# First attention with its two half-seen key blocks merged into one before the softmax

## The reference, cut to what matters

```python
scores = jnp.einsum('bqhgd,bshd->bhgqs', qg, k) * sm_scale
allowed = (j <= i) & (j > i - SLIDING_WINDOW)
scores = jnp.where(allowed[None, None, None], scores, neg)
attn = jax.nn.softmax(scores, axis=-1)
out = jnp.einsum('bhgqs,bshd->bqhgd', attn, v).reshape(B, S, N_Q_HEADS * HEAD_DIM)
return out @ wo
```

## Time and profile before

| what | before |
|---|---|
| median of 3 runs | 2206.22 us (2202.36 to 2208.6) |
| the profiled execution: its own time | 2204.66 us |
| its span, first to last instruction | 2202.8 us |
| mean granted TensorE clock | 0.995 |
| first attention, passes of `kv_head` | about 62 to 692 us of the span |

### The profile page before, as it was taken

One profiled execution on the slowest core, in us unless ns is written; L12 is line 12 of the kernel. 1 busy time (PEld: TensorE's weight loads), 2 busy tenths in 40 slices (PEclk: granted clock), 3 DMA queues, 4 the chain that ended last, 5 costly groups with the idle time before them and its releaser, 6 DMA issues.

```text
span 2202.8 us, 41666 instructions
## 1 busy us (share of the span) xinstructions
PE 2151.4 (98%) x11084; PEld 1653.8 (75%) x11084; DVE 1700.4 (77%) x3415; ACT 1460.7 (66%) x2868; POOL 1232.4 (56%) x1091
## 2 busy tenths in 40 slices
PE   7999999999999999999999999999999999999988
PEld 5888888888887657777777777777777777777756
DVE  6777777777777668888888888888888877788865
ACT  3444444445444668888888888888888877777742
POOL 5656655665653446666666666666666620455334
PEclk9999999999999999999999999999999999999999
DMA  7011010010004142111111111111111111433341
GB/s 245 20 48 30 19 48 29 19 48 29 19 10 125 40 176 82 43 48 49 46 49 42 49 46 48 42 49 46 49 42 48 47 49 42 124 92 111 87 126 39
DMA packets 125422, 132.20 MB, mean 60 GB/s; under 512 B 33205, under 2 KB 75733, under 8 KB 125348
## 3 DMA queue, kind: packets, MB, share of 16 engines
q1 hardware_dynamic: 121508, 118.70, 18.1%
q0 software_dynamic: 3840, 12.59, 1.9%
HBM read 101.46 MB, written 29.10 MB: 59 GB/s over the span
## 4 chain that ended last, share of the span: by engine, by line
PE 92%; DVE 4%; ACT 1%; SPq 1%; issue 1%; POOL 0%; DMA 0%; DVEq 0%; ACTq 0%; POOLq 0%
PE bank L2464 12%; PE bank L2451 11%; PE bank L2471 11%; PE bank L2036 9%; PE bank L2038 9%; PE bank L2037 9%; PE bank L2492 6%; PE bank L2383 5%; PE bank L2382 5%; PE bank L2381 5%; PE bank L2489 2%; PE bank L2172 2%; DVE rope_b L1535 1%; DVE rope_b L1536 1%; DVE rope_a L1534 1%
## 5 line engine op out<-in xcount | busy, mean ns | idle before, releaser
L1817 DVE TENSOR_REDUCE mcol<-bank 128x1 fp32r<-128x512 f32 x1024 | 693.9, 689 | 221.6 <-PE bank L2451 211.2
L2464 PE MATMUL bank<-q,k 128*128 128x512 f32 x1024 | 418.8, 409 | 0.1
L2451 PE MATMUL bank<-km,q 128*128 128x512 f32 x1024 | 405.7, 397 | 2.9 <-DVE mcol L1817 1.6
L2471 PE MATMUL bank<-q,k 128*128 128x512 f32 x1024 | 406.2, 397 | 0.0
L2451 PEld LDWEIGHTS bank<-km,q 128*128 128x128 f32 x1024 | 316.2, 309 | 52.3 <-DVE mcol L1817 4.2
L1329 ACT ACTIVATE pT<-bank 128x512 f32<-128x512 f32 x512 | 284.5, 600 | 81.6 <-PE bank L2471 77.8
L1329 ACT ACTIVATE x<-bank 128x512 f32<-128x512 f32 x512 | 284.6, 600 | 80.8 <-PE bank L2471 77.0
L2464 PEld LDWEIGHTS bank<-q,k 128*128 128x128 f32 x1024 | 192.2, 188 | 127.0 <-ACT x L1329 44.3
L2471 PEld LDWEIGHTS bank<-q,k 128*128 128x128 f32 x1024 | 192.3, 188 | 32.4
L2383 PE MATMUL bank<-hT_hi,wr_lo 128*128 128x512 f32 x512 | 202.9, 396 | 0.0
L2381 PE MATMUL bank<-hT_hi,wr_hi 128*128 128x512 f32 x512 | 200.7, 392 | 1.6 <-DVE k L1690 1.6
(11 more groups left out here) (348 smaller groups left out, 5045.6 us busy)
## 6 DMA issues: line engine op xcount, KB each, us to landing
wst<-in_L_attn_Wq_rope SPq DMA_DIRECT2D x64, 256.0 KB, 3.0
o_d<-ost SPq DMA_DIRECT2D x504, 32.0 KB, 1.8
st_q<-in_L_attn_wq SPq DMA_DIRECT2D x8, 1024.0 KB, 7.4
st_wo<-in_L_attn_wo SPq DMA_DIRECT2D x8, 1024.0 KB, 5.2
km<-kc_d SPq DMA_DIRECT2D x256, 32.0 KB
q<-qc_d SPq DMA_DIRECT2D x256, 32.0 KB
k<-kc_d SPq DMA_DIRECT2D x256, 32.0 KB
wm<-in_L_wmod SPq DMA_DIRECT2D x6, 1024.0 KB, 9.3
```

The source lines that it names most:

```text
L1817: dve.tensor_reduce(mcol[:, k % 2, i % 4, i // 4:i // 4 + 1], bank[4 + i % 2][:], AX.X, ALU.max, negate=True)\
L2451: pe.matmul(bank[4 + i % 2][:], q2[:, k % 4, h, i % 4:S:4], km[:, b, h], start=True, stop=True).then_inc(max_mm, 1)
L2464: pe.matmul(bank[s % 4][:], k1[:, k % 2, t], q1[:, k % 4, h], start=True, stop=False)
L2471: pe.matmul(bank[s % 4][:], k2[:, k % 2, h, t], q2[:, k % 4, h], start=False, stop=True).then_inc(scores1, 1)
```

## The change

The two half-seen blocks are merged while the scores are in the banks: where the first block's place is not seen, the second block's score is copied over it (`copy_predicated`, predicate from the window mask read as integers). From then on a slot has 128 columns a head, not 256. Maximum, exponential and normalising work on the banks; the exponential is written back into the bank. One block is turned, into bank 2 or 3 by the parity of qb. The turned weights P hold both blocks; the output is V_before * P + (V_own - V_before) * (P where own), so the differences of neighbouring V blocks (`dv_hi`, `dv_lo`) are made once a pass, and `pT_hi[:, 1]`, `pT_lo[:, 1]` are P's parts times the 0/1 tile `own` (on DVE and on POOL). There are still six matmuls a slot. For qb = 0 the mask stays as it was; the exponential reads `probs` and writes the bank. `scores` now waits for `probs0` (normalised) of the slot before, not for `masked0`. The lists of `kv_head` are reordered on all four engines, and the last pass on DVE; SP loads one more tile of 64 KB (`own`), and some small tiles change place in SBUF. The second layer's wait on `kr_split` becomes one on `kv_split`.

```diff
 POOL
+            def own_weights(slot):
+                mine = own[:].unsqueeze(1).broadcast_to([P, GQ, P])
+                pool.wait_ge(pT_split, 2 * slot + 1)
+                pool.tensor_tensor(heads(pT_lo[:, 1]), heads(pT_lo[:, 0].bitcast(F32)), mine, ALU.mult).then_inc(pT_split, 1)
 ACT
+            def dv_high(half, b):
+                act.wait_ge(proj_free, TURNS * half + TURN["Vt"] + 1)
+                wait(act, pv0, 4 * half)
+                act.activation(dv_hi[:].rearrange("p t d -> p (t d)"), vT[:, 0:3 * P], ACT.Copy).then_inc(v_hi_done, 1)
...
-                    e = act.activation(probs[:, i, h, c], probs[:, i, h, c], ACT.Exp, bias=nmax[:, i, h:h + 1], scale=-1.0,
-                                       accum_out=den[:, i, h:h + 1])
+                    ps = bank[h // 2][:, at:at + P]
+                    e = act.activation(ps, probs[:, i, h, P:2 * P] if qb == 0 else ps, ACT.Exp, bias=nmax[:, i, h:h + 1],
+                                       scale=-1.0 if qb == 0 else float(HD) ** -0.5, accum_out=den[:, i, h:h + 1])
...
-                for kb in range(1 if qb == 0 else 0, 2):
-                    e = act.activation(pT_hi[:, kb], bank[2 + kb][:], ACT.Copy)
+                act.activation(pT_hi[:, 0], bank[2 + qb % 2][:], ACT.Copy).then_inc(pT_hi_done, 1)
 DVE, evacuate "Vt"
-                    dve.tensor_tensor(v_lo[:, b].rearrange("p t d -> p (t d)"), ps[:], v_hi[:, b]...,
-                                      ALU.subtract).then_inc(proj_free, 1)
+                    dve.tensor_tensor(flat(v_lo[:, b]), ps[:, 0:3 * P], flat(v_hi[:, b]).bitcast(F32), ALU.subtract)
+                    dve.tensor_tensor(later, ps[:, P:4 * P], flat(v_hi[:, b]).bitcast(F32), ALU.subtract).then_inc(kv_split, 1)
+                    dve.wait_ge(kv_split, 2 * half + 1)
+                    dve.tensor_tensor(later, later, flat(v_lo[:, b]).bitcast(F32), ALU.subtract).then_inc(proj_free, 1)
 DVE
+            def dv_low(half, b):
+                dve.wait_ge(v_hi_done, 2 * half + 2)
+                dve.tensor_tensor(dv_lo..., vT[:, 0:3 * P], dv_hi..., ALU.subtract).then_inc(kv_split, 1)
 DVE, mask, qb > 0
-                for h in range(GQ):
-                    e = dve.tensor_tensor_reduce(probs[:, i, h, c], ps[:, c], window[:, c], -(float(HD) ** -0.5), 3e38, ALU.add, ALU.min,
-                                                 nmax[:, i, h:h + 1])
+                seen = window[:, 0:P].bitcast(U32).unsqueeze(1).broadcast_to([P, 2, P])
+                for j in range(2):
+                    e = dve.copy_predicated(score_block(j, 0), seen, score_block(j, 1))
+                e.then_inc(masked0, 1)
+                peak = bank[0][:, P:P + GQ]
+                dve.wait_ge(masked0, 3 * slot + 1)
+                for j in range(2):
+                    e = dve.tensor_reduce(peak[:, 2 * j:2 * j + 2], score_block(j, 0), AX.X, ALU.max, negate=True)
+                e.then_inc(masked0, 1)
+                dve.wait_ge(masked0, 3 * slot + 2)
+                dve.tensor_scalar(nmax[:, i], peak, scale, None, ALU.mult).then_inc(masked0, 1)
 DVE, normalise
-                dve.tensor_tensor(probs[:, i, :, c], probs[:, i, :, c], rden[:, i].unsqueeze(2).broadcast_to([P, GQ, n]), ALU.mult)
+                for j in range(2):
+                    heads = slice(2 * j, 2 * j + 2)
+                    e = dve.tensor_tensor(probs[:, i, heads, kb * P:(kb + 1) * P], score_block(j, kb),
+                                          rden[:, i, heads].unsqueeze(2).broadcast_to([P, 2, P]), ALU.mult)
 DVE, weights_low
-                for kb in range(1 if qb == 0 else 0, 2):
-                    e = dve.tensor_tensor(pT_lo[:, kb], bank[2 + kb][:], pT_hi[:, kb].bitcast(F32), ALU.subtract)
+                if qb > 0:
+                    dve.tensor_tensor(heads(pT_hi[:, 1]), heads(bank[2 + qb % 2][:]), own[:]..., ALU.mult)
+                dve.tensor_tensor(pT_lo[:, 0], bank[2 + qb % 2][:], pT_hi[:, 0].bitcast(F32), ALU.subtract)\
+                   .then_inc(pT_split, 2 if qb == 0 else 1)
 PE, scores
-                wait(pe, masked0, slot)
+                wait(pe, probs0, slot)
 PE, transposes
-                wait(pe, pT_split, slot)
-                for kb in range(1 if qb == 0 else 0, 2):
-                    for h in range(GQ):
-                        e = pe.transpose(bank[2 + kb][:, h * P:(h + 1) * P], probs[:, qb % 2, h, kb * P:(kb + 1) * P], ident[:])
+                wait(pe, pT_split, 2 * slot - 2 if qb == 2 else 2 * slot - 3)
+                for h in range(GQ):
+                    e = pe.transpose(bank[2 + qb % 2][:, h * P:(h + 1) * P], probs[:, qb % 2, h, c], ident[:])
 PE, sum_values
+                pe.matmul(bank[4][:], v_hi[:, b, at], pT_hi[:, 0], start=True, stop=False)
+                pe.matmul(bank[4][:], v_hi[:, b, at], pT_lo[:, 0], start=False, stop=False)
+                e = pe.matmul(bank[4][:], v_lo[:, b, at], pT_hi[:, 0], start=False, stop=(qb == 0))
+                if qb > 0:
+                    pe.wait_ge(pT_split, 2 * slot + 2)
+                    pe.matmul(bank[4][:], dv_hi[:, at], pT_hi[:, 1], start=False, stop=False)
+                    pe.matmul(bank[4][:], dv_hi[:, at], pT_lo[:, 1], start=False, stop=False)
+                    e = pe.matmul(bank[4][:], dv_lo[:, at], pT_hi[:, 1], start=False, stop=True)
```

More of the change, by code:

```diff
@@ L7 @@
 F32R = mybir.dt.float32r
+U32 = mybir.dt.uint32
 I32 = mybir.dt.int32
@@ L151, in adaln_two_layers @@
         gate_f0 = sb0("gate_f0", [P, B, D])
+        with ExitStack() as first:
+            sbs = sbuf_in(first)
+            cT = sbs("cT", [P, 2, B, KT])
+            silu_e = sbs("silu_e", [P, 2, B, KT])
+            silu_d = sbs("silu_d", [P, 2, B, KT])
+        dv_lo = sb0("dv_lo", [P, TB - 1, HD], F32R)
         qT_hi, qT_lo = (bq0_hi, bq1_hi), (bq0_lo, bq1_lo)
@@ L1130, in kv_head @@
                         weights_high0(n + 1, 3)
+                    out_high(slot + 2)
+                    rope_high(half + 1, "Q3", nb)
+                    weights_high(slot + 3, 3)
+                    dv_high(half + 1, nb)
                     out_high(slot + 3)
@@ L1548, in mask @@
-                e.then_inc(masked0, 1)
+                if qb == 0:
+                    c = slice(P, 2 * P)
+                    for h in range(GQ):
+                        ps = bank[h // 2][:, (h % 2) * 2 * P:(h % 2 + 1) * 2 * P]
+                        e = dve.tensor_tensor_reduce(probs[:, i, h, c], ps[:, c], window[:, c], -scale, 3e38, ALU.add, ALU.min,
+                                                     nmax[:, i, h:h + 1])
+                    e.then_inc(masked0, 3)
+                    return
@@ L1602, in kv_head @@
                     evacuate(half + 1, "Q0", nb)
+                    normalise(slot + 1, 1)
                     evacuate(half + 1, "Q1", nb)
+                    weights_low(slot + 1, 1)
+                    mask(slot + 2, 2)
                     out_low(slot)
-                    normalise(slot + 1, 1)
-                    mask(slot + 2, 2)
-                    weights_low(slot + 1, 1)
                     evacuate(half + 1, "Vt", nb)
+                    normalise(slot + 2, 2)
+                    evacuate(half + 1, "Q2", nb)
                     gate_attention(slot, b)
-                    normalise(slot + 2, 2)
+                    mask(slot + 3, 3)
                     out_low(slot + 1)
-                    evacuate(half + 1, "Q2", nb)
-                    mask(slot + 3, 3)
                     weights_low(slot + 2, 2)
@@ L1623, in kv_head @@
                     mask(slot + 4, 0)
+                    gate_attention(slot + 2, b)
+                    dv_low(half + 1, nb)
                     out_low(slot + 3)
+                    normalise(slot + 4, 0)
                     if not last:
                         evacuate(half + 2, "V", b)
-                    normalise(slot + 4, 0)
             norm_stats(0, 0)
@@ L1706, in _ @@
             out_low(4 * LAST)
+            normalise(4 * LAST + 2, 2)
+            mask(4 * LAST + 3, 3)
             merged_low(1)
-            mask(4 * LAST + 3, 3)
-            normalise(4 * LAST + 2, 2)
             norm_rows(1, 0)
@@ L2254, in kv_head @@
                     project_out(slot + 2, n)
+                    scores(slot + 4, half + 1, nb, 0)
                     sum_values(slot + 3, half, b, 3)
-                    if isinstance(n, int) and n == 0 and b == 0:
-                        pe.wait_ge(gate_ready, 1)
-                    scores(slot + 4, half + 1, nb, 0)
                     if not last:
```

113 lines of the change are left out of this document (63 added, 50 removed).

## The result

The changed kernel takes **2210.95 us** (median of 14 runs, 2207.97 to 2216.34), before takes 2205.45 (median of 14, 2202.36 to 2208.6): a ratio of 1.0029, with a 95% interval of 1.0020 to 1.0038. The forecast was 2195, in a range of 2184 to 2209. The profiled execution of the changed kernel took 2216.21 us, which is 5.3 above its median, its span is 2214.4 (before 2202.8), its mean granted clock 0.991 (before 0.995).

What follows compares the result with a forecast made beforehand. TensorE, busy 98% of the span, was taken as the bound. Fifteen passes -20.0, last pass +7.5, clock +1.7, start +0.4 sum to -10.4: 2194.3 from the profiled 2204.66, forecast as 2195 us, range 2184 to 2209.

Steps and rivals of the forecast that it cites:

- twelve at 0.2275: TensorE, Q1 in a pass: twelve matmuls at 0.2275 us each, 2.73 in all, within the 8.68 before values 1.
- Transposes, -1.30 a pass: TensorE: four fewer turns in each of three slots, 12 x 0.109 = 1.30 us a pass off.
- The old wait, -0.75: TensorE between Q1 and Q2: values 0 and transposes 1 cover the wait before Q2, -0.75 us a pass.
- What is late next, +0.72: Values 1 waits for oT_lo: VectorE's chain 9.30 against TensorE's 8.68, a 0.62 wait plus 0.1, +0.72 a pass.
- A second place without slack. Nothing is lost.: project_out 1 needs slot 1's oT_lo: 2.66 on VectorE against Q3's 2.73 on TensorE, nothing lost, 0.07 left.
- some 1.3 a pass, hidden: VectorE: the V differences add some 1.3 us a pass; its total stays 31 to 32 of 41, below TensorE.
- The last pass: Scores 2 and 3 wait for a whole softmax: +3.8 and +5.0, with the turns' -1.3, +7.5 us.
- The clock, +1.7: Last pass: one of the two new waits lowers TensorE's clock, +1.7 us, with 0 and 3.4 as ends.
- The start, +0.4 (0 to 1.2): Before the first rotary product: one more 64 KB tile and a V evacuation longer by 0.8, +0.4 us.
- the first (a copy of two turns): Rival: VectorE's predicated copy in a bank takes 0.69, not 0.34; 21 us more, 2216, slower; chance 0.11.
- The third (no waits): Rival: VectorE keeps up, the new waits stay away, a pass loses all of 2.05; 2183 us; chance 0.12.
- the chain is dearer in small pieces: Rival: bank writes, handoffs, a late GpSimd product cost 0.4 to 0.9 a pass; 2200 to 2208, no change; chance 0.20.

Runs made afterwards that it cites:

- e9: Changed kernel, orders untouched, with nmax and den moved to the end of the first layer's tiles, putting tiles on a multiple of 256 bytes again: 2201.77 us.
- e8: Changed kernel with VectorE's swaps in a pass, a reordered last pass, and nmax and den moved behind dv_lo: 2181.15 us.
- e1_moved: Kernel before, with only cT, silu_e and silu_d moved behind gate_f0, so nearly every tile behind ident lies 192 bytes lower: 2217.05 us.
- e3: Changed kernel with three swaps in VectorE's list of a pass: oT_lo ahead of the masks of slots 2 and 3, and of dv_low: 2196.95 us.
- e15: Kernel before, with only hT_hi and hT_lo 64 bytes higher, all weights as before modulo 256: 2212.23 us.

## Why the prediction was wrong

It was 16 us too low. The step that failed is the one that let every matmul that stays keep its length, "twelve at 0.2275", and the second layer its time, with nothing in the sum for the small tiles that change place. That is 9.2 of the 16 (changed kernel less e9), in no term and in no rival. Without it the kernel is 2201.77, inside the range, 6.8 above the forecast. Between landmarks, e9's profile has 15.7 less than before over the 14 passes (18.6 were forecast), 10.3 more from the last Vt to ffn (7.5, and 1.7 for the clock, were forecast), 3.1 more at the start, of which 1.1 is the late first projection, and nothing from ffn to the end. By steps:

- *Transposes, -1.30 a pass.* Right: 1.41 in place of 2.73, 1.31 less.
- *The old wait, -0.75.* Right: scores 2 to Q2 takes 1.51 in place of 2.15, and Q2's slow first matmul is gone (e8: 2.75 in place of 2.86).
- *What is late next, +0.72.* Right in place and releaser. VectorE's chain, from Q0's last matmul to the first of values 1, was to be 9.30; it is 9.26 (360.02 to 369.28). TensorE's side was to be 8.68 and is 8.85 with the slow steps, so the wait was smaller, 0.41 with 0.08 for its first matmul; in e9 it is 0.59 and 0.1.
- *"A second place without slack. Nothing is lost."* The slack of 0.07 was none. In e9 project_out 1 takes 2.83 in place of 2.72, so 0.11 is lost.
- *Not in the sum: `dv_low` ahead of `oT_lo` of slot 3.* It was costed inside "some 1.3 a pass, hidden". In the changed kernel it takes 0.55 to 1.74 us, median 1.48, and project_out 3 loses 0.15 a pass on average in e9. What stands ahead of an instruction that TensorE waits for is not hidden because its engine has idle time elsewhere. These two places, 0.26, are about what e9's 1.12 falls short of 1.33: 3 us in fifteen passes.
- *The addresses, 0 assumed.* Failed: 0.23 a pass net in the changed kernel (40.96 to 41.19), 0.43 in e1_moved where no wait absorbs any, and some 6 us from ffn to the end. "The second layer takes as long as before" was the sentence that the trace refuted first.
- *The last pass.* "Waits of about 3.5 and 5 us": scores 2 start 6.0 after scores 1 end (687.38), where 6.2 was summed; scores 3 start 11.1 after scores 2, where 9.7 was summed, and 1.3 of the 1.4 is scores 2 itself, 2.73 long at the lower clock in place of 1.42. Not in the sum: the wait for `oT_lo` at the end of the fifteenth pass, 1.79 in before, is 2.70; e3's order has 1.88 there.
- *The clock, +1.7.* Too small: it fell behind both waits. The windows 691.80 to 698.60 and 705.50 to 708.90 have a granted clock of 0.50, the lower level, with TensorE busy 5.21 and 3.40 us of them, where before had 1.00. Half of that busy time, 4.3, is an estimate of the work lost; 1.3 of it is the longer scores 2 above. The prediction had 3.4 as an end. It had named the Trainium skill (TensorE: Matmul & The Clock Gate, "What's actually happening"), by which both waits cost it and the sum is 1.7 higher: by that rule, the traces agree.
- *The start, +0.4 (0 to 1.2).* Right for the code (0.4 to 0.6), but the wait that grew from 0.50 to 1.5 brings the clock down in some executions, 1.6 more.

Of the rivals, the first (a copy of two turns) falls: copies are 0.34 apart. The third (no waits) falls too. The second, "the chain is dearer in small pieces", has 2200 to 2208, and e9's 2201.77 lies in it, but by luck in the main: VectorE's chain before values 1 was as long as summed, and only the 0.11 at project_out 1 is of its kind; `dv_low`, the clock and the start are not. None had a cost outside the changed stages.

The page that the prediction names beside rival 1, of the Trainium skill, gives VectorE one PSUM read port. Copies 0.34 apart, as fast as the old mask with its one bank input, are what that port allows if the old value is not read: by that rule, the trace agrees. The rule alone did not decide; the 0.34 did, and no run shows how the old value is kept.

## What to carry to other kernels

When a change adds, removes or moves a tile, compare where weights and moving operands of the long matmul chains lie against each other modulo 256 bytes, and restore the distance before judging the change; a group whose mean rose by 1% in a stage that nobody touched is a sign to look, though not yet a loss: in e15 such a mean rose and the stage took no longer. In each engine's list look at what stands directly ahead of an instruction that the bound engine waits for, and put optional work (here the mask, `dv_low`) behind it: three such swaps gave 11 us in fifteen passes. Where the bound engine has to wait, count the clock as well.
